# Down products in plain fp32; the gate is copied out by ScalarE and weighted by GpSimd

## The reference

```python
xn = layernorm(x)
# attention: 16 heads of 8 channels, rotary q and k, softmax, then Wout and bout
attn = (softmax(rope(q) @ rope(k).T / sqrt(8)) @ v) @ Wout + bout
# feed-forward on the same xn: one shared expert and 16 routed ones, top 2
r = sigmoid(xn @ gate_w + gate_b);  v, i = top_k(r, 2);  v = v / v.sum()
hg, hu = xn @ experts_wg, xn @ experts_wu            # per expert, 64 wide
ffn = xn + mlp(xn, shared) + sum_j v_j * ((silu(hg) * hu) @ experts_wd)[i_j]
out = x + attn + ffn
```

## Time and profile before

| what | value |
|---|---|
| median of 3 runs | 239.06 us (238.88 to 239.64) |
| the profiled execution's own time | 239.08 us |
| its span, first to last instruction | 237.2 us |
| granted TensorE clock, mean | 0.984 of full speed |
| busy: PE, PEld, DVE, ACT, POOL | 90%, 58%, 79%, 57%, 69% of the span |

### The profile page before, as it was taken

The page is one execution under the profiler, slowest core; times in us unless marked ns, Lnnn a source line. Parts: engine busy times, 40 slices in busy tenths (PEclk is TensorE's granted clock), DMA queues, the critical chain, the costliest instruction groups (busy, mean ns, idle before and its releaser), DMA issues.

```text
span 237.2 us, 4808 instructions
## 1 busy us (share of the span) xinstructions
PE 212.7 (90%) x1603; PEld 138.2 (58%) x1603; DVE 186.9 (79%) x407; ACT 135.3 (57%) x253; POOL 162.5 (69%) x245
## 2 busy tenths in 40 slices
PE   0485698889999999999999999999999999999993
PEld 0254454365565666665755656766766666676651
DVE  5897959999886888999858778998688878876521
ACT  2476111244458656665574766667676767666662
POOL 9185764799825479968938586979885874648722
PEclk9998789999999999999999999999999999999999
DMA  7924444630537340503662423206425550311101
GB/s 224 368 69 141 115 141 131 194 121 0 164 95 220 92 136 5 155 0 94 199 195 58 149 59 104 53 26 192 135 61 166 170 153 9 91 41 52 48 3 44
DMA packets 35953, 26.53 MB, mean 112 GB/s; under 512 B 4236, under 2 KB 30156, under 8 KB 35916
## 3 DMA queue, kind: packets, MB, share of 16 engines
q1 hardware_dynamic: 35292, 25.33, 35.9%
q10 hardware_dynamic: 636, 0.88, 1.0%
HBM read 18.53 MB, written 7.47 MB: 110 GB/s over the span
## 4 chain that ended last, share of the span: by engine, by line
PE 64%; DVE 18%; DMA 5%; SPq 4%; issue 3%; ACT 3%; POOL 1%; DVEq 0%; ACTq 0%; POOLq 0%
PE PV L553 11%; PE S2b L534 6%; PE S2a L534 5%; PE S1a L513 4%; DVE mx L1019 4%; PE S1b L513 4%; PE FB L391 3%; PE FA L393 3%; PE FA L391 3%; PE FA L392 3%; PE FB L393 3%; PE Y L391 3%; PE FB L392 3%; PE Y L392 2%; PE Y L393 2%
## 5 line engine op out<-in xcount | busy, mean ns | idle before, releaser
L749 ACT ACTIVATE probs<-S2b 128x512 f32<-128x512 f32 x62 | 37.0, 596 | 31.0 <-PE S2b L534 30.8
L1154 POOL TENSOR_TENSOR hid_lo<-gu,hid_hi 128x512 fp32r<-128x512 f32 (+1 forms) x27 | 34.7, 1286 | 23.5 <-ACT hid_hi L792 21.7
L1019 DVE TENSOR_REDUCE mx<-S1b 128x2 f32<-128x512 f32 x63 | 43.1, 684 | 7.8 <-PE S1b L513 7.7
L1019 DVE TENSOR_REDUCE mx<-S1a 128x2 f32<-128x512 f32 x65 | 44.5, 684 | 5.7 <-PE S1a L513 5.7
L1138 POOL TENSOR_TENSOR gu<-gu,wbc 128x512 f32<-128x512 f32 x32 | 41.0, 1282 | 11.5 <-DVE gu L1007 9.2
L749 ACT ACTIVATE probs<-S2a 128x512 f32<-128x512 f32 x62 | 37.1, 599 | 14.3 <-PE S2a L534 11.7
L553 PE MATMUL PV<-probs,vx 128*32 128x256 f32 x512 | 35.0, 384 | 0.9 <-ACT probs L749 0.9
L761 ACT ACTIVATE th<-FA 128x512 f32<-128x512 f32 (+1 forms) x36 | 21.5, 596 | 25.1 <-PE FA L393 24.8
L1028 DVE SCALAR_TENSOR_TENSOR th<-th,FA 128x512 f32<-128x512 f32 (+1 forms) x36 | 24.6, 683 | 10.9 <-ACT th L761 10.1
L513 PE MATMUL S1a<-k_hat,q_hat 96*128 96x256 bf16 x130 | 25.3, 275 | 0.7 <-DVE mx L1019 0.7
L513 PE MATMUL S1b<-k_hat,q_hat 96*128 96x256 bf16 x126 | 24.3, 273 | 1.4 <-DVE mx L1019 1.3
(11 more groups left out here) (171 smaller groups left out, 437.8 us busy)
## 6 DMA issues: line engine op xcount, KB each, us to landing
wbc<-route_w SPq DMA_DIRECT2D x64, 128.0 KB, 3.0
q_hat<-q_parts SPq DMA_DIRECT2D x32, 96.0 KB, 2.6
k_hat<-k_parts SPq DMA_DIRECT2D x32, 96.0 KB, 2.6
k_parts<-parts SPq DMA_DIRECT2D x8, 192.0 KB, 2.1
q_parts<-parts SPq DMA_DIRECT2D x8, 192.0 KB, 2.2
x_sb<-in_x SPq DMA_DIRECT2D x4, 256.0 KB, 4.1
q_parts<-parts SPq DMA_DIRECT2D x8, 128.0 KB, 2.1
k_parts<-parts SPq DMA_DIRECT2D x8, 128.0 KB, 2.1
```

Of the source, the lines that this page charges most:

```text
L749: nc.scalar.activation(probs[:, head % (2 * NQ), :], exp_bank(head)[:], ACT.Exp, scale=SCALE).then_inc(exp_done, 1)
L1019: nc.vector.tensor_reduce(mx[:, (q // QB) % 2, (q // 2) % 2, :, q % 2, i], S1[use % 2][:].rearrange("p (t s) -> p t s", t=SB), axis=AX.X, ...
L1154: nc.gpsimd.tensor_tensor(hid_lo[0:rows, m % 2, :], gu[0:rows, m % GU_SLOTS, :], hid_hi[0:rows, m % 2, :].bitcast(f32), ALU.subtract).then ...
```

## The change

All 36 down products become the plain fp32 matmul of `gu` and one unsplit copy of the down weights, which now lie in a buffer of their own (`wd_sb`). The roundings `hid_hi`, the differences `hid_lo`, the splits of the down weights and their semaphores go, and so do SyncE's waits for them. From chunk 6 on (`GATES_COPIED`) ScalarE copies the gate's product out of FA right behind its tanh, VectorE no longer makes `(th + 1) * FA` but does `(th + 1) * FB` where it multiplied by FB, and GpSimd makes two products: gate times routing weight, and `gu` times that.

```diff
-PLAIN = NCH
+GATES_COPIED = CHLEAD
...
-        wd_hi, wd_lo = sb("wd_hi", [P, NCH, C], f32r), sb("wd_lo", [P, NCH, C], f32r)
+        wd_sb = sb("wd_sb", [P, NCH, C])
...
-                if g == 1 and GT * (c + 1) > 2 * (1 + E) * I:
-                    sp.wait_ge(down_done, NCH)
-                    sp.wait_ge(down_split, NCH)
...
-                if n < PLAIN:
-                    pe.wait_ge(gu_weighted, n + 1)
-                    nc.tensor.matmul(Y[:], wd_sb[0:rows, c, :], gu[0:rows, n % GU_SLOTS, :],
-                                     start=c == 0, stop=c == NCH - 1).then_inc(down_done, 1)
-                    return
-                if n == PLAIN:
-                    pe.wait_ge(down_split, NCH)
-                pe.wait_ge(hid_ready, n + 1 - PLAIN)
-                split_product(Y[:], wd_hi[0:rows, c, :], wd_lo[0:rows, c, :], hid_hi[0:rows, n % 2, :],
-                              hid_lo[0:rows, n % 2, :], c == 0, c == NCH - 1).then_inc(down_done, 1)
+                pe.wait_ge(gu_weighted, n + 1)
+                nc.tensor.matmul(Y[:], wd_sb[0:rows, c, :], gu[0:rows, n % GU_SLOTS, :],
+                                 start=c == 0, stop=c == NCH - 1).then_inc(down_done, 1)
...
-            act.wait_ge(ld_down, 32)
-            nc.scalar.activation(wd_hi[0:I, 0, :], wd_sb[0:I, 0, :], ACT.Copy)
-            nc.scalar.activation(wd_hi[:, 1:, :], wd_sb[:, 1:, :], ACT.Copy).then_inc(down_hi_ready, 1)
...
                         nc.scalar.activation(th[0:rows, n % 2, :], FA[0:rows, :], ACT.Tanh, scale=0.5).then_inc(th_ready, 1)
+                        if n >= GATES_COPIED:
+                            if n - 2 >= GATES_COPIED:
+                                act.wait_ge(gu_weighted, n - 1)
+                            nc.scalar.activation(gate[0:rows, n % 2, :], FA[0:rows, :], ACT.Copy,
+                                                 scale=0.5 if n % NCH == 0 else 1.0).then_inc(fa_read, 1)
...
-                    if i == 2 and PLAIN <= n - 1 < LAST_ROUNDINGS:
-
-                        rows = I if (n - 1) % NCH == 0 else P
-                        act.wait_ge(gu_weighted, n)
-                        if n - 3 >= PLAIN:
-                            act.wait_ge(down_done, n - 2)
-                        nc.scalar.activation(hid_hi[0:rows, (n - 1) % 2, :], gu[0:rows, (n - 1) % GU_SLOTS, :],
-                                             ACT.Copy).then_inc(hid_hi_ready, 1)
...
-                        nc.vector.tensor_tensor(gu[0:rows, m % GU_SLOTS, :], FB[0:rows, :], th[0:rows, m % 2, :],
-                                                ALU.mult).then_inc(fb_read, 1)
+                        if m < GATES_COPIED:
+                            nc.vector.tensor_tensor(gu[0:rows, m % GU_SLOTS, :], FB[0:rows, :], th[0:rows, m % 2, :],
+                                                    ALU.mult).then_inc(fb_read, 1)
+                        else:
+                            nc.vector.scalar_tensor_tensor(gu[0:rows, m % GU_SLOTS, :], th[0:rows, m % 2, :], 1.0,
+                                                           FB[0:rows, :], ALU.add, ALU.mult).then_inc(fb_read, 1)
...
-                    if i == 0 and n < NCHUNKS:
+                    if i == 0 and n < GATES_COPIED:
...
-                    if i == 2 and LAST_ROUNDINGS <= n - 1 < NCHUNKS:
-                        round_hidden(n - 1)
...
+            def weight_gate_and_product(m):
+
+                g, c = chunk_group(m)
+                rows = I if c == 0 else P
+                gates, product = gate[0:rows, m % 2, :], gu[0:rows, m % GU_SLOTS, :]
+                pool.wait_ge(fa_read, A_USE["hg", m] + 1)
+                if c:
+                    pool.wait_ge(wbc_ld[c - 1], 32 * (g + 1))
+                    after(nc.gpsimd.tensor_tensor(gates, gates, wbc[:, g % 2, c - 1, :], ALU.mult))
+                pool.wait_ge(fb_read, B_USE["hu", m] + 1)
+                nc.gpsimd.tensor_tensor(product, product, gates, ALU.mult).then_inc(gu_weighted, 1)
...
-                if 0 <= m < NCH:
-                    down_low(m)
-                if PLAIN <= m < NCHUNKS:
-                    rows = I if m % NCH == 0 else P
-                    pool.wait_ge(hid_hi_ready, m + 1 - PLAIN)
-                    nc.gpsimd.tensor_tensor(hid_lo[0:rows, m % 2, :], gu[0:rows, m % GU_SLOTS, :],
-                                            hid_hi[0:rows, m % 2, :].bitcast(f32), ALU.subtract).then_inc(hid_ready, 1)
```

More of the change, by code:

```diff
@@ L74 @@
 FOUR_BANKS = NBLK - 2
-LAST_ROUNDINGS = NO_MAXIMA + CHLEAD - 1
 ROUTE_FIRST = (0, 0, 3, 3, 3, 3, 3)
@@ L198, in layer_kernel @@
         th = sb("th", [P, 2, GT])
+        gate = sb("gate", [P, 2, GT])
         gu = sb("gu", [P, GU_SLOTS, GT])
-        hid_hi, hid_lo = sb("hid_hi", [P, 2, GT], f32r), sb("hid_lo", [P, 2, GT], f32r)
         yT = sb("yT", [P, 2, GT])
@@ L215, in layer_kernel @@
         wg_sb, wu_sb = stage[:, 0:(1 + E) * I], stage[:, (1 + E) * I:2 * (1 + E) * I]
-        wd_sb = stage[:, 2 * (1 + E) * I:2 * (1 + E) * I + NCH * C].rearrange("p (c d) -> p c d", c=NCH)
         S1 = [ps("S1a"), ps("S1b")]
@@ L939, in attention_half @@
                                                rden_half.unsqueeze(3).broadcast_to([P, SB, 2 * NQ, D]), ALU.mult)
-            def round_hidden(m):
-                dve.wait_ge(gu_weighted, m + 1)
-                dve.wait_ge(down_done, m - 1)
-                nc.vector.tensor_copy(hid_hi[:, m % 2, :], gu[:, m % GU_SLOTS, :]).then_inc(hid_hi_ready, 1)
             def read_b(kind, g):
@@ L1111, in xt_low, with weight_product @@
                                         ALU.subtract).then_inc(xlo_ready, 1)
-            def down_low(c):
-                rows = I if c == 0 else P
-                if c == 0:
-                    pool.wait_ge(down_hi_ready, 1)
-                nc.gpsimd.tensor_tensor(wd_lo[0:rows, c, :], wd_sb[0:rows, c, :], wd_hi[0:rows, c, :].bitcast(f32),
-                                        ALU.subtract).then_inc(down_split, 1)
+            def weight_product(m):
+                g, c = chunk_group(m)
+                pool.wait_ge(fb_read, B_USE["hu", m] + 1)
+                if c == 0:
+                    nc.gpsimd.tensor_scalar(gu[0:I, m % GU_SLOTS, :], gu[0:I, m % GU_SLOTS, :], 0.5, 1.0,
+                                            ALU.mult, ALU.mult).then_inc(gu_weighted, 1)
+                else:
+                    pool.wait_ge(wbc_ld[c - 1], 32 * (g + 1))
+                    nc.gpsimd.tensor_tensor(gu[:, m % GU_SLOTS, :], gu[:, m % GU_SLOTS, :], wbc[:, g % 2, c - 1, :],
+                                            ALU.mult).then_inc(gu_weighted, 1)
+            def weight_gate_and_product(m):
+                g, c = chunk_group(m)
+                rows = I if c == 0 else P
+                gates, product = gate[0:rows, m % 2, :], gu[0:rows, m % GU_SLOTS, :]
+                pool.wait_ge(fa_read, A_USE["hg", m] + 1)
+                if c:
+                    pool.wait_ge(wbc_ld[c - 1], 32 * (g + 1))
+                    after(nc.gpsimd.tensor_tensor(gates, gates, wbc[:, g % 2, c - 1, :], ALU.mult))
+                pool.wait_ge(fb_read, B_USE["hu", m] + 1)
+                nc.gpsimd.tensor_tensor(product, product, gates, ALU.mult).then_inc(gu_weighted, 1)
             pool.wait_ge(parts_done[0], 2 * PARTS)
@@ L1129, in _ @@
                     negate_maxima(negated_half(blk))
-                if 0 <= m < NCHUNKS:
-                    g, c = chunk_group(m)
-                    pool.wait_ge(fb_read, B_USE["hu", m] + 1)
-                    if c == 0:
-                        nc.gpsimd.tensor_scalar(gu[0:I, m % GU_SLOTS, :], gu[0:I, m % GU_SLOTS, :], 0.5, 1.0,
-                                                ALU.mult, ALU.mult).then_inc(gu_weighted, 1)
-                    else:
-                        pool.wait_ge(wbc_ld[c - 1], 32 * (g + 1))
-                        nc.gpsimd.tensor_tensor(gu[:, m % GU_SLOTS, :], gu[:, m % GU_SLOTS, :], wbc[:, g % 2, c - 1, :],
-                                                ALU.mult).then_inc(gu_weighted, 1)
+                if 0 <= m < GATES_COPIED:
+                    weight_product(m)
+                elif GATES_COPIED <= m < NCHUNKS:
+                    weight_gate_and_product(m)
                 for kind, g in late_a(blk):
```

9 lines of the change are left out of this document (5 added, 4 removed).

## The result

The changed kernel takes 242.63 us (median of 4 runs, 242.40 to 243.04), the kernel before 239.08 us on the same chip (238.88 to 239.64). The ratio is 1.0147, 95% interval 1.0125 to 1.0169: slower by 3.5 us. The forecast was 240.5 us, so the direction was right. But the rise is more than double of the 1.4 us that were forecast, and the time lies just above the range of 239.0 to 242.6 us. Its profiled execution took 242.69 us, with a span of 240.0 us, 2.8 us above the span before. In the groups of the experiments the kernel before itself ran between 238.4 and 242.5 us, so differences under 1 us are read from the traces and not from medians.

The account below looks back on a forecast made before the run. TensorE was taken to set about 100 us, handing over with VectorE in 32 us. Costs of 4.05 less 2.65 recovered (1.37 + 0.53 + 0.75) gave net 1.4 us, so 240.5 us; range 239.0 to 242.6 us.

Parts of the forecast that it names:

- GpSimd's new product: On GpSimd, 27 products of gate and weight (34.6 us) replace subtractions, running while it waits for gu; counted at nothing.
- TensorE, 4.05 us: 27 down products, chunks 9 to 35, go from 0.71 to 0.86 us on the chain: 4.05 us more.
- four full passes: Rival on TensorE's down products: a plain product costs 0.95 us, giving 242.8 us; chance 0.02.
- The wait at 112 us: TensorE's transpose waits for gu behind layernorm steps slowed beside a hid_lo; 0.53 us recovered, bounds 0 and 0.53.
- the stall at 130 us: TensorE's wait at 130.72 us, from ScalarE's rounding waiting for GpSimd, goes; 0.75 us recovered, bounds 0 and 0.75.
- the 0.42 at 57 us: TensorE's wait at 57.04 us before transposes of the maxima, recovered through VectorE's relief: 0.42 us.
- VectorE's relief, 1.37 us: VectorE loses 30 steps th; worth only what TensorE waits for VectorE, 1.37 us recovered.
- The waits at 104.06 us: TensorE's wait for VectorE before transposes of the maxima, counted in VectorE's relief as 0.25 us.
- ScalarE's copies at nothing: 30 gate copies (17.9 us) replace 24 roundings (15.2 us), covered by ScalarE's idle of 0.80 us; no cost counted.
- Nothing back: Rival: the gate's copy makes exponentials late and new waits replace the old ones, 243.1 us; chance 0.12.
- the signs of being right: Y at 0.86 us, blocks 0.15 us longer, VectorE about 70% busy, no waits at 130.72 and 112.09, exponentials awaiting S2b.
- the signs of being wrong: New TensorE idle of a microsecond, probs delayed by the copy, late q and k loads, or a shorter 161 to 224 us.

Follow-up runs that it names:

- e2: Changed kernel with down products from chunk 9 on as three fp32r matmuls, hidden values rounded once, the third matmul repeating the first; 240.66 us, ratio 1.0027.
- e11: Changed kernel, down products from chunk 9 as two fp32r matmuls without hidden's low part, GpSimd waiting in three places for VectorE's steps; 233.03 us, ratio 0.9708.
- e8: Changed kernel without GpSimd's product of gate and routing weight, ScalarE's copies kept; 241.37 us, ratio 1.0078.
- e6: Changed kernel with plain down products alone, the gate left with VectorE and GpSimd as before; 241.65 us, ratio 1.0074.
- e5: The changed kernel itself, run again beside others on one chip; 244.08 us, ratio 1.0179 to the kernel before.
- e9: e6 with two more GpSimd products in block 3, whose results nothing uses; 241.54 us, ratio 1.0067.
- e12: e9 with a small GpSimd product between the two extra ones, so the last starts later; 242.6 us, ratio 1.0151.

## Why the prediction was wrong

The step that failed is the term for GpSimd's new product, which the sum has at nothing. The runs show 1.74 us in its place, from the first to the last PV product. The terms one by one:

- **TensorE, 4.05 us: right.** Y stands at 0.86 us on the chain in nearly every block, TensorE's blocks grew by about 0.15 us each, and e2 gave them back. The 0.95 us of the rival with four full passes didn't come; why it is 0.86 no run shows.
- **The wait at 112 us (0.53) and the stall at 130 us (0.75): right.** Xn at 110.98 us takes 1.17 us, and both waits are gone in every kernel without the roundings but e11, which has 0.31 us of the first. They were even undersized. (The four xn of 2.26 us had not one GpSimd instruction beside them, as the prediction reads it, but two: the last step of a split, `parts`, which ran until 109.51 us, and behind it the `hid_lo`.) The blocks there, from which I expected 0.15 us more, are 0.61 and 0.86 us shorter, 1.77 us in all. Steps of the router beside a `hid_lo` lay on the path as well: `wsel` took 1.44 us at 101.87 and 0.77 us at 154.12. With the four other blocks of the table 2.92 us came back in this part, and I had put 2.23 there (2.65 less the 0.42 at 57 us).
- **VectorE's relief, 1.37 us: the cause is wrong.** "It is worth what TensorE waits for VectorE, and no more." From 57 us on it was worth nothing (174.01 us in e8, 174.02 in e6). The waits at 104.06 us and before the first-pass scores in the router's stretches did go, but in e6 as well, where VectorE keeps every `th`. They came from steps that a `hid_lo` held, and not from VectorE having too much to do. That as much came back as the sum has, though for another cause, is luck in this term. The wait at 57.04 us did not go; it grew to 1.18.
- **GpSimd's new product at nothing: wrong, and the costly one.** "The new product can run in the time in which GpSimd now waits for `gu`." It did run there. But this was the time in which VectorE made its steps with all operands in SBUF undisturbed. I had the mechanism in hand, from xn at 109.09 us, counted it where a product went, and did not look at what lay under the place where one came. I wrote that it is 0.53 us "if one falls there again", and left that out of the sum and the range. It cost 0.97 + 0.80 us in these two blocks. The 0.76 us more in the wait at 57 us I don't count: in the profiled execution `resid` held the step there, not the new product, and TensorE had come to that wait 0.83 us earlier than before, so that the first PV product started 0.08 us earlier. (In e5 it was the gate product at 56.41 us that held `wtok`.)
- **ScalarE's copies at nothing: right.** e8 keeps them all.

The rivals that lie nearest to 242.63 us by number are not what happened either. Nothing back (243.1 us) fails by the 2.92 us that came back, and four full passes (242.8 us) by the 0.86 us. All the signs of being right that the prediction names came, too: Y, the blocks, VectorE at 70%, the two waits. None of them looked at the steps that the new product could hold. Of the signs of being wrong one came, an idle TensorE (0.79 us at 69.75) in a stretch that had none.

The Trainium skill (SBUF — State Buffer, Who interferes with whom) names both kinds of step that were held here: `tensor_scalar`, when it runs in a two-port mode, and a VectorE instruction with two inputs in SBUF against a GpSimd instruction that reads SBUF. It excludes `tensor_reduce`. By this rule, the trace agrees for the first two, with 2.15 for 1.11 us and 1.19 for 0.23 us. The `tensor_reduce` steps here, `mx`, read PSUM and so don't test the rule; none of the 128 took over 0.70 us. Applied to the new product's place in the timeline before, where GpSimd is idle beside xn, the rule would have pointed at the loss in advance.

In numbers: 4.05 - 2.92 + 1.74 = 2.87 us from the first to the last PV product, -0.08 ahead of it, and 2.8 us in the spans. Of these the 4.05 is reckoned and the 2.92 its remainder; the others are measured. The medians say 3.55 us. The three other executions of the changed kernel had spans of 240.5 to 240.6 us, and the time outside the span was 2.7 us in the profiled one, where before it was 1.9. I have not traced that rest. In e5 the median stood 4.66 us above before, and its profile had the first PV product 1.6 us later than the first profile of the same kernel. So up to 1 or 2 us of the difference in the medians may lie ahead of 58 us or behind the last instruction. What sets the executions apart there stays open.

## What to carry to other kernels

When work is moved onto an idle engine, look at what the other engines do in that idle time: GpSimd's was idle because VectorE was in its SBUF steps, and filling it made a relieved VectorE late at two places. Count the collisions that an edit makes by the same row that shows you those it takes away. Before giving an engine relief, ask whether the waits on it are from its load or from a step that something holds; the second kind goes with the holder.

## What the runs showed of the hardware

- A VectorE step with its operands in SBUF, held by a GpSimd instruction, loses what this has left, less 0.26 us here (0.43 of 0.69, 0.84 of 1.10). The GpSimd instruction takes no longer for it (1.26 to 1.28 us in e9 and e12).
- VectorE steps that read PSUM were not held: `gu<-th,FB` took 0.66 to 0.69 us in all its 30 runs in the changed kernel, `mx` at most 0.70.
- A group of short instructions can be held more than once: four xn took 3.20 us in e2, with three GpSimd instructions let in.
- Even the smallest steps of the router are held: `tsel` (128x8) took 0.76 us at 102.61 in the changed kernel beside a GpSimd product, and 0.15 us in e6 with none beside it.

```profile
102.08 1.27 POOL L1114 TENSOR_TENSOR gu<-gu,gate 128x512 f32<-128x512 f32 x1
102.61 0.76 DVE L855 SCALAR_TENSOR_TENSOR tsel<-top,den 128x8 f32<-128x8 f32 x1
```

- The last 128 KB stores landed 1.7 us after their issue in the first profile of the changed kernel and 2.4 us in that of e5, in the median of two, with the same instructions. The span ends 2.2 us and 3.4 us behind the last issue (237.84 and 239.39 us).
